# A state-space layer whose product with the C row moves from VectorE to GpSimd

## The reference, cut to what matters

```python
def step(h, t):
    dA_t, dBx_t, C_t = t
    h = dA_t * h + dBx_t
    return (h, jnp.einsum('ben,bn->be', h, C_t))
_, ys = jax.lax.scan(step, h0, (dA..., dBx..., Cm...))
y = ys.transpose(1, 0, 2) + D_skip * xc
y = y * jax.nn.silu(z)
return y @ W_out.T
```

## Time and profile before

| | before |
|---|---|
| median of 3 runs | 1696.12 us (1695.65 to 1700.82) |
| the profiled execution | 1696.32 us, its span 1694.5 us |
| busy: PE, DVE | 1251.0 us (74%), 1175.1 us (69%) |
| busy: ACT, POOL | 606.9 us (36%), 395.3 us (23%) |
| granted TensorE clock, mean | 0.826 |

### The profile page before, as it was taken

How to read it: one execution, slowest core, us unless ns; L and a number is a source line. 1 busy time by engine, 2 the same in 40 slices (tenths; PEclk the granted TensorE clock), 3 DMA queues, 4 the chain that set the end, 5 groups by cost and what they waited for, 6 DMA issues and landing times.

```text
span 1694.5 us, 13336 instructions
## 1 busy us (share of the span) xinstructions
PE 1251.0 (74%) x4026; PEld 619.1 (37%) x4026; DVE 1175.1 (69%) x2595; ACT 606.9 (36%) x1086; POOL 395.3 (23%) x284
## 2 busy tenths in 40 slices
PE   2222775966487675967696887878889789999897
PEld 1001332332233222343232553635547345555554
DVE  6897798878987898847547688696785752444321
ACT  1510652236322642224232331412233325764543
POOL 5232042312422142211103223030320111111211
PEclk8555886979697986969797679797787989999999
DMA  5000000000000000020001000000000010000000
GB/s 178 0 0 0 1 1 0 1 0 1 0 1 1 0 0 1 1 85 1 1 0 56 1 1 0 1 1 1 1 1 1 0 56 1 7 1 7 1 7 7
DMA packets 11271, 17.78 MB, mean 10 GB/s; under 512 B 1304, under 2 KB 7584, under 8 KB 10688
## 3 DMA queue, kind: packets, MB, share of 16 engines
q1 hardware_dynamic: 11200, 16.93, 2.9%
HBM read 15.88 MB, written 1.05 MB: 10 GB/s over the span
## 4 chain that ended last, share of the span: by engine, by line
PE 33%; DVE 14%; ACT 4%; issue 2%; POOL 1%; POOLq 0%; DVEq 0%; ACTq 0%
PE bankE L1659 7%; PE bankE L1737 4%; PE bankE L1149 4%; PE bankE L1132 3%; DVE b_yt L1454 2%; PE bankE L1151 1%; PE bankS L1701 1%; PE bankE L518 1%; PE bankS L1686 1%; ACT b_pr L1046 1%; DVE c_tw L1829 1%; PE bankE L544 1%; DVE b_xnS L1236 1%; PE bankE L1134 1%; DVE b_pT L1426 1%
## 5 line engine op out<-in xcount | busy, mean ns | idle before, releaser
L284 POOL TENSOR_TENSOR cv<-cv,hc 128x1024 f32<-128x1024 f32 x60 | 141.4, 2357 | 303.9 <-DVE hc L683 303.6
L676 DVE TENSOR_TENSOR_SCAN hs<-dA,carry,dbx 128x512 f32<-128x512 f32 x128 | 186.0, 1493 | 3.9 <-ACT dA L358 0.5
L1659 PE MATMUL bankE<-c_h,c_w 128*128 128x512 f32 x288 | 151.7, 609 | 9.5 <-DVE c_tw L1829 6.6
L1632 ACT ACTIVATE c_h<-bankE,C 128x512 f32<-128x512 f32 x144 | 98.9, 688 | 117.4 <-PE bankE L1737 117.2
L395 ACT ACTIVATE sg<-bankE,C 128x512 f32<-128x512 f32 x80 | 54.9, 687 | 172.5 <-PE bankE L518 172.5
L1829 DVE SCALAR_TENSOR_TENSOR c_tw<-bankE,C,wb_ready 128x512 f32<-128x512 f32 x32 | 24.0, 750 | 130.0 <-PE bankE L1659 130.0
L449 PE MATMUL bankS<-bc,sel 96*128 96x512 bf16 x64 | 30.5, 476 | 102.5 <-DVE hc L683 89.5
L1737 PE MATMUL bankE<-c_fH,c_w1H 128*128 128x512 f32 x144 | 100.8, 700 | 0.0
L1046 ACT ACTIVATE b_pr<-bankE,b_nm 128x160 f32<-128x160 f32 x128 | 48.4, 404 | 139.3 <-DVE b_nm L1415 139.3
L1149 PE MATMUL bankE<-b_kTt,b_qT 64*128 64x160 f32 x256 | 85.9, 424 | 9.4 <-ACT b_pr L1046 8.8
L358 ACT ACTIVATE dA<-dl,Aneg 128x512 f32<-128x512 f32 x128 | 81.1, 709 | 26.6 <-DVE hs L676 26.4
(11 more groups left out here) (478 smaller groups left out, 2829.3 us busy)
## 6 DMA issues: line engine op xcount, KB each, us to landing
c_w<-in_w SPq DMA_DIRECT2D x1, 2304.0 KB, 8.7
X<-in_x SPq DMA_DIRECT2D x4, 256.0 KB, 3.8
wg<-in_gate_T SPq DMA_DIRECT2D x1, 1024.0 KB, 7.9
wu<-in_up_T SPq DMA_DIRECT2D x1, 1024.0 KB, 10.0
f<-in_w SPq DMA_DIRECT2D x1, 1024.0 KB, 7.3
out<-X SPq DMA_DIRECT2D x4, 256.0 KB, 2.3
b_wq<-in_Wqkv SPq DMA_DIRECT2D x1, 768.0 KB, 4.9
g<-in_sw SPq DMA_DIRECT2D x2, 256.0 KB, 3.5
```

The source lines that it names most:

```text
L284: pool.tensor_tensor(cv[:, :, :], cv[:, :, :], hc[:, k % 2, :, :], ALU.add).then_inc(s["y_acc"], 1)
L676: V.tensor_tensor_scan(hs[:, h, :], dA[:, (HV * k + h) % DA, :], dbx[:, h, :], carry[:, k, h:h + 1], ALU.mult, ALU.add).then_inc(s["scan_d ...
L1632: act.activation(h[:, n % 3, :], E[k % 2][:, :], ACT.Gelu_apprx_tanh, bias=col("b1_3", k)).then_inc(s["c_h"], 1)
L1659: pe.matmul(E[2][:, :], w2[:, k, :], h[:, n % 3, :], start=(f == 0), stop=(f == FB3 - 1)).then_inc(s["c_down"], 1)
```

## The change

It touches the piece o, its neighbours, and the order of all pieces.

```diff
@@ memory
-MAMBA_END = 125920
+MAMBA_END = 134112
-    hs = sb("hs", [P, HV, G])
-    hc = sb("hc", [P, 2, HV, G])
+    HS = 3
+    hs = sb("hs", [P, HS, HV, G])
+    hc = sb("hc", [P, HV, G])
+    cb = sb("cb", [P, 2, G])
-    XA = sb2("XA", [P, NG * T * P])
+    XA = sb2("XA", [P, 2 * T * P])
@@ gpsimd
             elif p[0] == "o" and k > 0:
+                weigh_state(i, k, hc)
                 at_least(pool, s["hc_ready"], i, NS, k + 1)
-                if k > 1:
-                    at_least(pool, s["y_acc"], i, NS - 1, k - 1)
-                pool.tensor_tensor(cv[:, :, :], cv[:, :, :], hc[:, k % 2, :, :], ALU.add).then_inc(s["y_acc"], 1)
+                pool.tensor_tensor(cv[:, :, :], cv[:, :, :], hc[:, :, :], ALU.add).then_inc(s["y_acc"], 1)
+            elif p == "o0":
+                weigh_state(i, 0, cv)
...
+        def weigh_state(i, k, dst):
+            at_least(pool, s["scan_done"], i, HV * NS, HV * (k + 1))
+            at_least(pool, s["cb_ready"], i, NS, k + 1)
+            if k > 1:
+                at_least(pool, s["y_acc"], i, NS - 1, k - 1)
+            pool.tensor_tensor(dst[:, :, :], hs[:, k % HS, :, :], cb[:, k % 2, :].unsqueeze(1).to_broadcast([P, HV, G]), ALU.mult).then_inc(s["hc_ready"], 1)
@@ scalar
+            elif p[0] == "N":
+                at_least(act, s["Cb_ready"], i, NS, k + 1)
+                at_least(act, s["hc_ready"], i, NS, k - 1)
+                act.activation(cb[:, k % 2, :], S[1][:, :], ACT.Copy).then_inc(s["cb_ready"], 1)
@@ tensor
             elif p[0] == "N":
                 if k > 0:
-                    at_least(pe, s["hc_ready"], i, NS, k)
+                    at_least(pe, s["cb_ready"], i, NS, k)
@@ vector
+                at_least(V, s["x2_done"], i - 1, 1)
...
                     if h == 0:
                         at_least(V, s["dbx_done"], i, NS, k + 1)
-                    V.tensor_tensor_scan(hs[:, h, :], dA[:, (HV * k + h) % DA, :], dbx[:, h, :], carry[:, k, h:h + 1],
+                        at_least(V, s["hc_ready"], i, NS, max(0, k + 1 - HS))
+                    V.tensor_tensor_scan(hs[:, k % HS, h, :], dA[:, (HV * k + h) % DA, :], dbx[:, h, :], carry[:, k, h:h + 1],
                                          ALU.mult, ALU.add).then_inc(s["scan_done"], 1)
             elif p[0] == "o":
                 at_least(V, s["scan_done"], i, HV * NS, HV * (k + 1))
-                at_least(V, s["Cb_ready"], i, NS, k + 1)
-                if k > 2:
-                    at_least(V, s["y_acc"], i, NS - 1, k - 2)
-                V.tensor_tensor(cv[:, :, :] if k == 0 else hc[:, k % 2, :, :], hs[:, :, :],
-                                S[1][:, :].unsqueeze(1).to_broadcast([P, HV, G]), ALU.mult).then_inc(s["hc_ready"], 1)
-                inc(V.tensor_copy(carry[:, k, :], hs[:, :, G - 1]))
+                inc(V.tensor_copy(carry[:, k, :], hs[:, k % HS, :, G - 1]))
```

More of the change, by code:

```diff
@@ L313, in scalar @@
         act.wait_ge(s["ld_x"], 32)
-        act.activation(Aneg[:, :], col("A_log", 0, HV * NS), ACT.Exp).then_inc(s["act_self"], 1)
-        act.wait_ge(s["act_self"], 1)
+        act.activation(Aneg[:, :], col("A_log", 0, HV * NS), ACT.Exp).then_inc(s["acts_const"], 1)
+        act.wait_ge(s["acts_const"], 1)
         act.activation(Aneg[:, :], Aneg[:, :], ACT.Copy, scale=-1.0).then_inc(s["acts_const"], 1)
         act.activation(sb2sum[:, :], col("sb2", 0), ACT.Identity, bias=col("sb2", 1)).then_inc(s["acts_const"], 1)
-        act.wait_ge(s["acts_const"], 2)
+        act.wait_ge(s["acts_const"], 3)
         act.wait_ge(s["consts"], 4)
@@ L996, in decay @@
             act.wait_ge(s["x1T_ready"], NG)
-            act.activation(wcol[:, 0:1], col("w"), ACT.Exp).then_inc(s["b_aself"], 1)
-            act.wait_ge(s["b_aself"], 1)
-            act.activation(wcol[:, 1:2], wcol[:, 0:1], ACT.Copy, scale=-1.0).then_inc(s["b_aself"], 1)
-            act.wait_ge(s["b_aself"], 2)
+            act.activation(wcol[:, 0:1], col("w"), ACT.Exp).then_inc(s["acts_const"], 1)
+            act.wait_ge(s["acts_const"], 4)
+            act.activation(wcol[:, 1:2], wcol[:, 0:1], ACT.Copy, scale=-1.0).then_inc(s["acts_const"], 1)
+            act.wait_ge(s["acts_const"], 5)
         def piece(p, i, e):
@@ L1435, in piece @@
                 norm("E", e, 1, tj(yt), tj(xnT))
-                add_to_x(e, xnT, "b_xc")
-                at_least(dve, s["b_xc"], e, 1, 1)
+                add_to_x(e, xnT, "x2_done")
+                at_least(dve, s["x2_done"], NG + e, 1, 1)
                 stats(xj(e), stE, mvE)
```

106 lines of the change are left out of this document (53 added, 53 removed).

## The result

| | before | after |
|---|---|---|
| median of 4 runs each | 1695.88 us (1692.82 to 1700.82) | 1743.98 us (1740.31 to 1748.09) |
| the profiled execution | 1696.32 us | 1740.31 us, its span 1738.5 us |
| granted TensorE clock, mean | 0.826 | 0.818 |

The changed kernel is slower: ratio 1.0281, 95% interval 1.0248 to 1.0315, or +48 us by the medians and +44.0 us between the two profiled executions. The forecast was +18.4 us. The direction and several of its steps came true, its size did not: the time lies above the 1728 of the forecast's own range, between the middle (1738) and the upper end (1745) of the rival in which GpSimd becomes a queue.

A forecast was written before the change was run, and what follows sets the result against it. DVE was taken to bound group 0, PE channels 10 to 14 and the part from 916 us. Terms 12.1 + 12.2 - 6.7 - 13.6 + 10 + 4.4 = +18.4 us on 1696.3 gave 1715, forecast range 1703 to 1728, whole range 1687 to 1745.

The forecast's parts named there:

- the rival in which GpSimd becomes a queue: Others wait behind POOL's products and additions, norms caught each time: +13.9 in channels 6 to 9, middle 1738 us; chance 0.22.
- Group 0: First 15 channels: scans and POOL's two instructions exclude each other, 6.8 us a channel, 99.7 against 87.6 us, +12.1.
- Channels 0 to 5: Later groups, channels with M pieces: DVE late to the scans, 7.1 us a channel plus `acc` sums, 140.7 against 128.5, +12.2.
- GpSimd's floor: In every channel, POOL's product and addition plus two scans, which exclude each other: 6.7 or 7.1 us by order.
- Channels 6 to 9: Later groups, norms and routers: DVE sheds 13.7 us of products, caught norms cost 7, net -6.7 (-13.7 to +13.9).
- Channels 10 to 14: Later groups, two U pieces for three: PE no longer bounds, DVE and POOL do at 7.1 us; 106.5 against 120.1, -13.6.
- Passages and ends: Between groups and at group ends: moved U pieces +10, product and addition both on POOL +4.4; together +14.4 us.
- The late part: From 916 us on only the order changes, PE busy 87% either way: 0, bounds -10 and +10 us.
- The C row at nothing: ACT's 64 copies of the C row, about 0.59 us each, cost nothing; 34.7 us of PE idle can go, uncounted.
- No exclusion for this product: Rival: scans keep 1.1 us while POOL multiplies, group 0 takes 4.8 us a channel (72.0); total 1629 us; chance 0.04.

The follow-up runs named there:

- the PSUM experiments: Scans read `dbx` from PSUM: group 0 only, kernel before 1690.16 us, changed kernel 1715.63; also half of later groups, 1675.14, 1686.01, with product on DVE 1674.23.
- the run with the edit for PSUM in group 0: Changed kernel with `dbx` of group 0 written to two PSUM banks, where the scans read it: 1715.63 us, one run.

## Why the prediction was right and wrong

**Group 0, +12.1 forecast, +9.3 measured.** Right in mechanism and cadence (6.7 to 7.1 forecast, 6.73 measured from the third channel on). The first two channels took 4.70 each, the time of one product and two scans. 13 x 6.73 + 2 x 4.70 = 96.9, where I had 99.7. The rule of the Trainium skill (SBUF — State Buffer, section "Who interferes with whom") names the interference, and the PSUM experiments here bear out its condition for scans, two SBUF inputs, with 1268 ns in group 0 against 1687 in the later groups of the same run. By its whole instruction a channel would take 7.1; measured is the shorter hand-over.

**Channels 0 to 5, +12.2 forecast, +12.7 measured.** The size is right, by luck in part: the run with the product on DVE and all else changed already gives +10.6 there, with DVE's idle time up from 4.2 to 11.8 us and its excess only from 13.0 to 16.2. So of the net +12.7 only 2.1 come with the product's move to GpSimd, whose price stands there against 18 products of relief, 20.5 us. The forecast gave it all to GpSimd's floor. How the rest of the change makes that idle time wasn't settled (the old order is no better there, 149.5).

**Channels 6 to 9, -6.7 forecast, +14.2 measured. This is the step that failed.** I took the 13.7 us of relief as coming through whole, because 11 us a channel is far above the floor of 7.1, and set only one price against it: 7 us for the norms, a quarter of "0 to 12 x 2.3 = 27.6". The norms did cost that: of the 21.7 us by which the excess grew, 7.3 are theirs. That the quarter came out is luck in part, as no row gave it. What failed is that scans and `carry` copies stood at nothing in this stretch. They cost 6.9 and 10.0 us more than before (2.4 of a router step that is no longer met go off). I looked for instructions special to the stretch, and forgot that each channel brings its own, and that a channel above the floor still pays when it is caught. The copy's row was in the earlier trace rows (0.32 us, "even for the small `carry` copy"), and I used it to choose the order of a channel but gave it no price. The measured price is 14.2 + 13.7 = 27.9 us: 21.7 of excess, 3.0 of idle time, and some 3.4 of M pieces that the new order moved in, which the sum didn't have either. The run with the product on DVE divides the 27.9: 3.7 are the rest of the change, 24.2 (10.5 measured and 13.7 of relief eaten up) are GpSimd's pass. Cutting the 12 products alone took 18.3 from the stretch.

**Channels 10 to 14, -13.6 forecast, -8.3 measured.** PE no longer bounds, as forecast (30.4 of 37.1 us busy). Mechanism and cadence came true: a steady channel takes 7.12 us, in the order in which the `carry` copy is caught behind the product, and 7.1 was the forecast. What was missed is mainly the first channel of the stretch, 8.64, 8.12 and 9.00 us in the three groups, 4.4 of the 5.3 us; what holds it wasn't tried. With the product on DVE a steady channel takes 6.4 us, so the floor of DVE and POOL is what bounds here.

**Passages and ends, +14.4 forecast, +9.2 measured.** In order of size right.

**The late part, 0 (-10 to +10) forecast, +6.9 measured.** From the last `dbx` on, the time goes with the granted clock of that part. The four kernels with the old order took 984.1, 986.8, 989.5 and 993.5 us at 0.872, 0.869, 0.863 and 0.858; the nine with the new one took 994.0 to 999.0 at 0.867 to 0.872, and up to 1007.6 at 0.860. So by number alone the two ranges meet, but at an equal clock the new order takes some 10 us longer (986.8 before, 997.0 after, both at 0.869), whichever engine has the product. Of these 10, 3.3 lie in the last group's end and 6.9 behind it, inside the forecast's bounds. Which of the moved pieces does it wasn't tried.

**The C row at nothing.** The time was right, but the reason thin: the 34.7 us of PE's idle time did go, and the kernel before with the new order shows that without ACT's copy 122.4 us would stand there. With the product on DVE channels 10 to 14 gain 22.8 us, which needs both the freed C row and the two U pieces in place of three (the new order without the copy took 123.3 us there), and GpSimd's pass takes 14.5 of them back.

**The rivals.** "POOL becomes a queue" was right in its result (1738) and half right in its mechanism: the caught norms are there, but the queue is not what costs most. It is DVE's own small and large instructions that stand still: cutting the addition, or giving the scans an input in PSUM, took off 83 and 28 us. That it came near is in part luck: its +13.9 for channels 6 to 9 meets the measured +14.2, but was to come from norms caught each time (27.6), and the norms cost 7.3. "No exclusion for this product" is excluded by the 6.73; the run with the edit for PSUM in group 0 shows what it would have been like there (72.9 us, that rival said 72.0).
